# A second weight pass for w3, moved token scales, and another rounding ladder in a transformer layer

## The reference, cut to what matters

```python
def _quant_input(x):                       # per token
    s = 127.0 / clip(max(|x|), 1e-5)
    return clip(round(x * s), -128, 127) / s

x  = x + attention(layernorm(x))
xq = _quant_input(layernorm(x))            # 2048 features
x13 = xq @ w13.T                           # 2 x 5632 features
x1, x3 = split(x13)
gated = relu(x1)**2 * x3
inner = gated * rsqrt(mean(gated**2) + 1e-5) * norm_w
iq = _quant_input(inner)                   # 5632 features
out = x + iq @ w2
```

## Time and profile before

| | value |
|---|---|
| median of 3 runs | 14608.73 us (14601.59 to 14653.77) |
| profiled execution, its own time | 14722.4 us |
| its span on the slowest core (core 4) | 14720.8 us |
| spans of cores 0 to 3 | 14501.2 to 14652.7 us |
| PE busy | 7258.6 us, 49% |
| DVE busy | 4725.8 us, 32% |
| ACT busy | 1681.4 us, 11% |
| POOL busy | 954.7 us, 6% |
| mean DMA rate | 37 GB/s |

### The profile page before, as it was taken

One profiled execution on the slowest core, in us unless ns is written; L12 is line 12 of the kernel. 1 busy time (PEld: TensorE's weight loads), 2 busy tenths in 40 slices (PEclk: granted clock), 3 DMA queues, 4 the chain that ended last, 5 costly groups with the idle time before them and its releaser, 6 DMA issues. The chain is left out here.

```text
span 14720.8 us, 55200 instructions; the slowest of 8 cores (14501.2 to 14720.8 us)
## 1 busy us (share of the span) xinstructions
PE 7258.6 (49%) x20055; PEld 2136.3 (15%) x20459; DVE 4725.8 (32%) x6802; ACT 1681.4 (11%) x2649; POOL 954.7 (6%) x816
## 2 busy tenths in 40 slices
PE   3475555666665666666552322277676721221304
PEld 1131111111111111111110100022222200110101
DVE  4425554111112111111213223322222255455463
ACT  0000000111111111111111001100000011111111
POOL 1000000000000000000001111100101000000010
PEclk7677777555555555555555655577878755666657
DMA  2232222000000000000011231111111102231304
GB/s 75 65 83 75 75 74 71 11 11 11 11 11 20 11 11 11 11 11 11 11 21 33 51 50 33 23 30 30 30 30 31 30 13 41 62 59 44 79 24 90
DMA packets 291561, 542.75 MB, mean 37 GB/s; under 512 B 91420, under 2 KB 190937, under 8 KB 270809
## 3 DMA queue, kind: packets, MB, share of 16 engines
q0 software_dynamic: 32192, 198.19, 7.8%
q1 hardware_dynamic: 245017, 311.64, 7.4%
q10 hardware_dynamic: 14080, 29.37, 0.7%
HBM read 617.74 MB, written 119.54 MB: 50 GB/s over the span
## 5 line engine op out<-in xcount | busy, mean ns | idle before, releaser
L1422 PE MATMUL o_ps<-iqT,w_sb 128*128 128x512 bf16 x2759 | 634.1, 388 | 2145.3 <-DMA w_sb<-w2w 2142.2
L818 DVE TENSOR_TENSOR probs<-probs,mask_sb 128x512 bf16<-128x512 bf16 x512 | 217.3, 424 | 3749.5 <-ACT probs L810 3749.5
L826 PE MATMUL av_ps<-probs,vh 128*128 128x512 bf16 x1231 | 748.2, 608 | 1201.6 <-DVE probs L818 630.4
L810 ACT ACTIVATE probs<-sc_ps,negc_bc 128x512 bf16<-128x512 f32 x1280 | 879.4, 687 | 3526.1 <-PE sc_ps L804 3526.1
L1200 PE MATMUL f_ps<-xqT,w_sb 128*128 128x512 bf16 x2756 | 887.9, 490 | 523.5 <-DMA w_sb<-w3w 516.2
L1393 DVE SCALAR_TENSOR_TENSOR a<-yq,a 128x512 f32<-128x512 f32 x1232 | 852.8, 692 | 42.0
L943 PE MATMUL o_ps<-at_sb,ow_sb 128*128 128x512 bf16 x1000 | 374.3, 551 | 962.1 <-DMA at_sb<-attnT_s 560.1
L804 PE MATMUL sc_ps<-qTr,kTr 64*128 64x512 bf16 x1280 | 773.1, 604 | 29.8 <-issue 29.8
L835 PE MATMUL r_ps<-probs,ones_st 128*1 128x512 bf16 x1280 | 747.3, 584 | 66.5 <-ACT probs L810 59.4
L797 PE MATMUL sc_ps<-qTn,kTn 128*128 128x512 bf16 x1217 | 738.7, 607 | 0.0
L1211 PE MATMUL f_ps<-xqT,w_sb 128*128 128x512 bf16 x2759 | 704.9, 410 | 4.1
(11 more groups left out here) (259 smaller groups left out, 7485.3 us busy)
## 6 DMA issues: line engine op xcount, KB each, us to landing
w_sb<-w2w POOLq DMA_DIRECT2D x64, 1408.0 KB, 11.5
xnb_t<-x_nat SPq DMA_DIRECT2D x32, 1024.0 KB, 7.3
xtb_c<-xT SPq DMA_DIRECT2D x128, 256.0 KB, 3.0
ow_sb<-ow POOLq DMA_DIRECT2D x64, 512.0 KB, 7.0
w_sb<-w1w POOLq DMA_DIRECT2D x44, 512.0 KB, 5.7
w_sb<-w3w POOLq DMA_DIRECT2D x44, 512.0 KB, 7.5
gw_s<-gw_t SPq DMA_DIRECT2D x176, 128.0 KB, 1.8
gw_c<-gw_s SPq DMA_DIRECT2D x176, 128.0 KB, 2.3
```

The costliest lines, as they stand in the source:

```text
L810: ex = p.op("s", lambda e, bank=bank, slot=slot: e.activation(probs[slot][:], sc_ps[bank][:], AF.Exp, bias=negc_bc[:], scale=1.0), deps=[m ...
L826: e.matmul(av_ps[:], vh[par][:, ci * 128:(ci + 1) * 128], probs[slot][:], start=(ci == 0), stop=(ci == n - 1), skip_group_check=True), dep ...
L1422: stop = p.op("t", lambda e, kc=kc, wp=wp: e.matmul(o5_ps[wp][:], w2_sb[wp][:, kc * 128:(kc + 1) * 128], iqT[:, kc * 512:(kc + 1) * 512], ...
```

## The change

Four edits:

1. **P3.** `xqT` now receives the whole numbers `r0 + sign * count` themselves: the product with `si_bc` is dropped (one DVE instruction less per feature chunk). Per token block two DVE products form the cube of the inverse scale in bf16, `si3_bc`.
2. **P4, weights.** The w3 chunk is loaded a second time as fp32 (`w3f_sb`, 1 MB, issued by SP), and DVE forms what the bf16 rounding lost, `w3l_sb = w3f_sb - w3_sb` (128 x 2048). Each w3 result is now 32 matmuls: 16 with `w3_sb` and 16 with `w3l_sb`, in the same accumulation.
3. **P4, product.** One more DVE instruction per token block and chunk multiplies the gated product by `si3_bc`; POOL's square waits for it. `cf_bc` is kept in bf16.
4. **P5.** The seven compare-and-add steps on the remainder's absolute value are replaced by six levels (128, 64, 32, 16, 8, 4), each a DVE comparison-times-weight and a POOL subtraction, one more POOL subtraction, four compare-and-add steps on DVE, and the product with the sign on POOL instead of DVE.

```diff
+            si3_bc = eb2(nc.sbuf_tensor("si3_bc", [128, MYB * 512], BF16))
...
+                    s3a = p.op("v", lambda e, blk=blk: e.tensor_tensor(
+                        si3f[:], si_bc[:], si_bc[:], ALU.mult), deps=[bsi, si3f_war])
+                    s3b = p.op("v", lambda e, blk=blk: e.tensor_tensor(
+                        si3_bc[:, blk * 512:(blk + 1) * 512], si3f[:], si_bc[:],
+                        ALU.mult), deps=[s3a])
...
-                        rf = p.op("v", lambda e, cp=cp: e.tensor_tensor(
-                            b_t[cp][:], b_t[cp][:], r0_t[cp][:], ALU.add), deps=[co])
                         xq = p.op("v", lambda e, dc=dc, cp=cp, gc0=gc0:
                                   e.tensor_tensor(
                                       xqT[:, dc * MYT + gc0:dc * MYT + gc0 + 512],
-                                      b_t[cp][:], si_bc[:], ALU.mult),
-                                  deps=[rf, bsi])
+                                      b_t[cp][:], r0_t[cp][:], ALU.add),
+                                  deps=[co])
...
-            cf_bc = eb2(nc.sbuf_tensor("cf_bc", [128, MYB * 512], F32))
+            cf_bc = eb2(nc.sbuf_tensor("cf_bc", [128, MYB * 512], BF16))
...
+                    wf = p.dma("q", f"wf{wpar}",
+                               w3f_sb[wpar][:].rearrange("p (c f) -> p c f", c=DCN),
+                               w3_h.ap()[fc], deps=[w3f_war[wpar]])
+                    w3l_tok[wpar] = p.op("v", lambda e, wpar=wpar: e.tensor_tensor(
+                        w3l_sb[wpar][:], w3f_sb[wpar][:], w3_sb[wpar][:],
+                        ALU.subtract), deps=[wf, w3_tok[wpar], w_war[wpar]])
+                    w3f_war[wpar] = w3l_tok[wpar]
...
-                        for dc in range(DCN):
-                            dd3 = [xq_tok[blk][dc], w3_tok[wpar]]
+                        for dcl in range(2 * DCN):
+                            dc, lo = dcl % DCN, dcl >= DCN
+                            dd3 = [xq_tok[blk][dc],
+                                   w3l_tok[wpar] if lo else w3_tok[wpar]]
...
+                                                  (w3l_sb if lo else w3_sb)[wpar][:, dc * 128:(dc + 1) * 128],
...
+                        g = p.op("v", lambda e, sp=sp, blk=blk: e.tensor_tensor(
+                            g_t[sp][:], g_t[sp][:],
+                            si3_bc[:, blk * 512:(blk + 1) * 512], ALU.mult),
+                            deps=[g])
...
-                        cm = p.op("v", lambda e, gp=gp: e.tensor_single_scalar(
-                            a_5[gp][:], yq5[gp][:], 0.5, ALU.is_gt), deps=[ab])
-                        for thr in (1.5, 2.5, 3.5, 4.5, 5.5, 6.5, 7.5):
+                        mbuf = [yq5[gp], a_5[gp], b_5[gp]]
+                        lv = ab
+                        for li, w in enumerate((128.0, 64.0, 32.0, 16.0, 8.0, 4.0)):
+                            mi = mbuf[li % 2 + 1] if li else mbuf[1]
+                            mp = mbuf[0] if li == 0 else mbuf[(li - 1) % 2 + 1]
+                            lv = p.op("v", lambda e, mi=mi, mp=mp, w=w:
+                                      e.tensor_scalar(mi[:], mp[:], w, w,
+                                                      ALU.is_gt, ALU.mult), deps=[lv])
+                            lv = p.op("g", lambda e, mi=mi, mp=mp:
+                                      e.tensor_tensor(mi[:], mp[:], mi[:],
+                                                      ALU.subtract), deps=[lv])
+                        u1 = p.op("g", lambda e, gp=gp: e.tensor_tensor(
+                            a_5[gp][:], yq5[gp][:], b_5[gp][:], ALU.subtract),
+                            deps=[lv])
+                        cm = u1
+                        for thr in (0.5, 1.5, 2.5, 3.5):
                             cm = p.op("v", lambda e, gp=gp, thr=thr:
                                       e.scalar_tensor_tensor(
-                                          a_5[gp][:], yq5[gp][:], thr, a_5[gp][:],
+                                          a_5[gp][:], b_5[gp][:], thr, a_5[gp][:],
                                           ALU.is_gt, ALU.add), deps=[cm])
-                        co = p.op("v", lambda e, gp=gp: e.tensor_tensor(
-                            b_5[gp][:], a_5[gp][:], d_5[gp][:], ALU.mult),
+                        rr = p.op("g", lambda e, gp=gp: e.tensor_tensor(
+                            a_5[gp][:], a_5[gp][:], d_5[gp][:], ALU.mult),
                             deps=[cm, sg])
```

More of the change, by code:

```diff
@@ L867, in build_nc @@
             cf_tok = [None] * MYB
+            SB2 = ExitStack()
+            eb2 = SB2.enter_context
+            si3_bc = eb2(nc.sbuf_tensor("si3_bc", [128, MYB * 512], BF16))
             with ExitStack() as P3:
@@ L892, in build_nc @@
                 si_bc = e3(nc.sbuf_tensor("si_bc", [128, 512], F32))
+                si3f = e3(nc.sbuf_tensor("si3f", [128, 512], F32))
                 tq = [e3(nc.sbuf_tensor(f"tq{i}", [128, 512], F32)) for i in range(2)]
@@ L915, in build_nc @@
                 mxtree_war = None
+                si3f_war = None
                 chain_war = [None, None]
@@ L1163, in build_nc @@
                          for i in range(2)]
+                w3l_sb = [e4(nc.sbuf_tensor(f"w3l_sb{i}", [128, DCN * 128], BF16))
+                          for i in range(2)]
+                w3f_sb = [e4(nc.sbuf_tensor(f"w3f_sb{i}", [128, DCN * 128], F32))
+                          for i in range(2)]
                 u_t = [e4(nc.sbuf_tensor(f"u_t{i}", [128, 512], F32)) for i in range(2)]
@@ L1171, in build_nc @@
                 w3_tok = [None, None]
+                w3l_tok = [None, None]
+                w3f_war = [None, None]
                 w_war = [None, None]
@@ L1205, in build_nc @@
                                                   skip_group_check=True), deps=dd1)
[L1206 to L1208 removed]
+                        for dcl in range(2 * DCN):
+                            dc, lo = dcl % DCN, dcl >= DCN
+                            dd3 = [xq_tok[blk][dc],
+                                   w3l_tok[wpar] if lo else w3_tok[wpar]]
+                            if dcl == 0:
                                 dd3.append(fps_war[p3b])
[L1210 removed]
+                            stop3 = p.op("t", lambda e, dc=dc, dcl=dcl, lo=lo, blk=blk,
+                                         wpar=wpar, p3b=p3b:
                                          e.matmul(f_ps[p3b][:],
[L1212 removed]
+                                                  (w3l_sb if lo else w3_sb)[wpar][:, dc * 128:(dc + 1) * 128],
                                                   xqT[:, dc * MYT + blk * 512:
                                                       dc * MYT + (blk + 1) * 512],
[L1215 removed]
+                                                  start=(dcl == 0), stop=(dcl == 2 * DCN - 1),
                                                   skip_group_check=True), deps=dd3)
@@ L1395, in build_nc @@
                                           ALU.is_gt, ALU.add), deps=[cm])
-                        co = p.op("v", lambda e, gp=gp: e.tensor_tensor(
-                            b_5[gp][:], a_5[gp][:], d_5[gp][:], ALU.mult),
+                        rr = p.op("g", lambda e, gp=gp: e.tensor_tensor(
+                            a_5[gp][:], a_5[gp][:], d_5[gp][:], ALU.mult),
                             deps=[cm, sg])
                         rf = p.op("v", lambda e, gp=gp: e.tensor_tensor(
-                            b_5[gp][:], b_5[gp][:], r0_5[gp][:], ALU.add), deps=[co])
+                            a_5[gp][:], a_5[gp][:], r0_5[gp][:], ALU.add), deps=[rr])
```

9 lines of the change are left out of this document (2 added, 7 removed).

## The result

| | before | changed |
|---|---|---|
| median of 10 runs | 14659.19 us (14601.59 to 14919.81) | 17446.15 us (17283.34 to 17696.68) |
| profiled execution, own time | 14722.4 us | 17424.22 us |
| its slowest core | core 4, 14720.8 us | core 3, 17422.7 us |

The changed kernel takes 1.186 times as long, with a 95% interval of 1.182 to 1.191. In some executions the cores of one die show a lower clock (0.608 to 0.611 against 0.630 to 0.633 in the one of 17696.68 us) and the time is longer (that one by 2.4% against the fastest); the medians contain such executions, the ratios and the profiled executions do not.

A forecast was written before the change was run, and what follows sets the result against it. No engine was full: P5 was taken as a serial chain, P4 as running on PE. P5 +1785 and +28, P3 -41, P4 +978 made +2750 us: 17,472, or 17,360 brought to the runs' median; range 17,050 to 17,800.

The forecast's parts named there:

- The P5 chunk: P5, the new ladder as one serial chain: 21.77 us a chunk against 11.63, +10.14, times 176 = +1785 us.
- rival A: P5: the two-operation comparison takes 0.69 instead of 0.43 us on 1056 instructions, +275, 17,635 us; chance 0.07.
- The w2 load: P5: issued behind the sign's product, so PE starts 9.2 us after the chunks; +7.0 us, four times, +28.
- P4, matmuls and product: P4, on PE's path: 16 more matmuls in each of 176 blocks, +611 us; the extra product, +127 us.
- P4, the third load: P4: the fp32 w3 load meets full DMA engines, 2.8 us in 43 chunks, +120 us (0 to +198).
- P4, half-clock starts: P4: the number of blocks starting at half clock can move either way; range -110 to +110 us.
- P4, the slowed clock: P4: matmuls at 0.263 instead of 0.217 us come more often; +120 us, between -73 and +263.
- Rival B: P4: the slowed clock holds throughout, +263 instead of +120, 17,500 us; chance 0.12.
- P3: the chain: P3: one DVE step of 0.73 us less in 64 chains, -47; two more per token block, +6; together -41 us.
- C: P5: DVE and POOL work on two chunks at once, POOL sets 11.4 us a chunk; 15,535 us; chance 0.01.
- D: P5: overlap deep enough to pay for all the rest, 6.1 us a chunk, 14,609 us or faster; chance 0.01.

The follow-up runs named there:

- the rearranged kernel before: Kernel before, arithmetic unchanged, with P5's chunks in pairs, first w2 loads early, one-column matmul one block later, next weight loads early: 13254.62 us, ratio 0.905.

## Why the prediction was right, point by point

**The P5 chunk: right.** Forecast +10.14 us a chunk and +1785; measured 21.74 - 11.63 = 10.11, times 176 = +1779. The open question, 0.43 or 0.69 us for the comparison with two operations, came out at 0.43, so rival A fell. The handovers were as in the chain of P3, 0.08 us towards POOL and 0.03 back.

**The w2 load: right.** It lands behind the chunks. PE starts 8.8 us after the chunks' end (mean of the four blocks of core 3) where it started 2.9 after them (core 4 before): 4 x 6.0 = +24 us against 28. Over all cores it is 9.1 against 2.4 us, +27.

**The matmul phases of P5: a term I left out.** The four phases took 830 us on core 3 and 703 on core 4 before: +127. Most of it is waiting for loads. Inside the phases PE sits idle 115 us for w2 on core 3, where it was 68 on core 4 before, and 42 more for DVE's `y2st`, which in turn waits for the load of `y1c` (none before). More matmuls run at half clock behind these gaps (259 stand 0.40 to 0.45 us apart, 143 on core 4 before), but hardly one at 0.263 us (3 on each; the granted clock is 0.81 nowhere in the phases), so it is not the slowed clock. The ladder does not cause it, since alone it leaves them at 177 to 192 us each, and the kernel before had 172 to 194. In the changed kernel they are 184 to 217, and the w2 loads land in 14.6 instead of 11.5 us on these two cores. Nor does anything else that P5 now does: the kernel without the low part has the whole changed P5, and took 175 to 195. One thing to look at are loads of two neighbouring cores that meet, counting each core's time from its own start: in the kernel before, pairs whose phases lie on each other for 0.95 to 0.97 of their time took 187 to 190 us a phase, pairs with 0.52 to 0.60 took 175 to 179. Cores 2 and 3 of the changed kernel have 0.98. But their 207 us a phase are more than any such pair before, and with the one-column matmul later cores 0 and 1 took 197 to 199 us a phase at 0.78. So the overlap is at most a part of it, and the cause stays open.

**P4, matmuls and product: right.** Forecast 611 + 127 = 738; a block grew from 9.36 to 13.54 us, times 176 = 736, and the two experiments that take one of them away return it.

**P4, the third load: right.** Forecast +120 (0 to 198), by the rate of plain copies; measured 113 to 118 for the wait itself; with the half-clock starts that went with it, taking the load away gave back 165.

**P4, half-clock starts: 0 forecast, about -65 measured.** The start in the earlier trace rows, 5.15 us for the 16 matmuls from 10507.95 to 10513.10, had a granted clock of 0.50 from 10509 to 10510, and 1.00 from 10513.1 on. On a core without slowed clock such starts cost 3.3 us a chunk before (core 1) and 1.8 after (core 5). The range held it, and I had named no sign.

**P4, the slowed clock: wrong.** Forecast +120 on core 4, where it had cost 73, because I assumed, with no row to show it, that matmuls in a larger share of the time would be slowed more often. They were slowed less: about 1530 matmuls of core 3 ran at 0.263 us, about 2430 of core 4 before, at 0.046 us each 70 and 112 us. On cores 4 to 7 it did not come at all. What core 3 loses against the unslowed core 5 is 117 us (3130 and 3013), what core 4 before lost against core 1 is 69 (2310 and 2241), net +48; but 26 of the 117 are a longer wait for weights, and the rest holds half-clock starts as well. With P4 the same and two chunks at once in P5 no core was slowed in P4, so no fixed price belongs to this term. Rival B, slowed throughout, fell. So P4 came to +820 instead of +978, and on cores 0 and 4 to 7 it took less than the 3100 us below which I had called the forecast wrong, for the clock or the third load; it was mostly the clock. On an unslowed core the sum is 736 + 104 (the load, core 5 against core 1) - 67 (starts) = 773, which is 3013 - 2241 + 1.

**P3: the chain right, the stage total no evidence.** A feature chunk takes 10.06 us where it took 10.79 on all eight cores, 64 times -0.73 = -47, as forecast. The stage as a whole does not show it: -31 over the cores' means, -2 on the two profiled cores. It differs by 100 us between cores of one kernel (1796 to 1896 before), and the rearranged kernel before, whose P3 is unchanged, is 113 us shorter in it on average than the kernel before.

**Rivals C and D fell** as argued: the queue holds a chunk complete. But the price that I gave C, 11.4 us a chunk, was wrong, as the run with two chunks at once shows. Even with the overlap built in, the comparison beside POOL's subtraction took 1.47 us instead of 0.43, and the pace was 17.4.

The total, +2702 between the profiled executions against +2750, is closer than its terms: 127 us left out of P5's matmul phases and 39 us that P3 did not fall stand against 158 too many in P4 and 50 us less in the stages that don't change. P5's chunk and w2 load and P4's matmuls, product and load were right by themselves; that 1.186 came so near to 1.188 is luck in the other terms.

## What to carry to other kernels

Before moving an elementwise step to an idle engine, find out whether its stage is bound by an engine or by a chain. In the chain of P5 every instruction counted at its full duration plus a handover, wherever it ran (1.26 us on POOL, 0.69 on DVE, handovers of 0.08 and 0.03), so the faster engine won even as the busier one (21.74 us a chunk down to 16.83). To fill the gaps, place independent work next in the queues (another chunk: 17.4 us a chunk instead of 21.74; the next block's matmuls: 10.77 us a block instead of 13.54), and check on one timeline that the two engines really run side by side.
